# DVE's order in the slots of an attention pair: the turn of exponentials ahead of the move of scores

## The reference

```python
q = x @ Wq.T + bq
p = softmax(q @ memory_keys.T / sqrt(128))          # 8192 x 4096
x = layernorm(x + (p @ memory_values) @ Wo.T + bo)
h = silu((x @ w1.T) * s1) * ((x @ w2.T) * s2)       # width 512
h = gelu((h @ h1.T) * s_h1)
h = gelu((h @ h2.T) * s_h2)
x = layernorm(x + (h @ w3.T) * s3)
```

## Time and profile before

| | |
|---|---|
| median of 3 runs | 1143.17 us (1141.53 to 1144.19) |
| profiled execution, its own time | 1143.68 us |
| its span, first to last instruction | 1141.9 us |
| attention, first frames | 0 to 117 us |
| attention, repeating pairs | 117 to 620 us |
| attention, last pairs | 620 to about 770 us |
| feed-forward | to the end |
| busy over the span | PE 96%, DVE 84%, ACT 79%, POOL 57% |

### The profile page before, as it was taken

How to read it: one execution, slowest core, us unless ns; L and a number is a source line. 1 busy time by engine, 2 the same in 40 slices (tenths; PEclk the granted TensorE clock), 3 DMA queues, 4 the chain that set the end, 5 groups by cost and what they waited for, 6 DMA issues and landing times. The chain is left out here.

```text
span 1141.9 us, 20141 instructions
## 1 busy us (share of the span) xinstructions
PE 1092.9 (96%) x5324; PEld 769.4 (67%) x5324; DVE 963.5 (84%) x1803; ACT 905.3 (79%) x1610; POOL 645.3 (57%) x618
## 2 busy tenths in 40 slices
PE   7799999999999999999999999988999999999996
PEld 5566666666666666666666666635787887888775
DVE  6888898998899889998998899875787887888874
ACT  6788788878887887788878877777788878888883
POOL 1487788878877887888778878760211121121110
PEclk9999999999999999999999999999999999999999
DMA  6878888888888888888888988854020111001000
GB/s 199 190 186 200 200 201 205 206 197 204 201 195 195 202 200 199 200 206 202 200 194 208 207 186 198 186 124 166 1 56 28 28 48 34 28 28 55 11 10 29
DMA packets 83942, 165.90 MB, mean 145 GB/s; under 512 B 19648, under 2 KB 47808, under 8 KB 83776
## 3 DMA queue, kind: packets, MB, share of 16 engines
q1 hardware_dynamic: 79824, 161.50, 59.8%
q10 hardware_dynamic: 4080, 3.94, 1.2%
HBM read 22.76 MB, written 8.39 MB: 27 GB/s over the span
## 5 line engine op out<-in xcount | busy, mean ns | idle before, releaser
L454 POOL TENSOR_TENSOR pT<-slot_p,pT 128x512 f16<-128x512 f32 x496 | 561.9, 1168 | 143.5 <-ACT pT L506 143.5
L608 DVE TENSOR_SCALAR_CACHE_REDUCE rows<-s_ps 128x1024 f32<-128x1024 f32 x256 | 310.8, 1214 | 72.9 <-DMA slot_p<-rows 48.3
L506 ACT ACTIVATE pT<-slot_p 128x512 f16<-128x512 f32 x512 | 296.1, 617 | 84.1 <-DMA slot_p<-rows 76.2
L577 DVE STREAM_TRANSPOSE rows<-rows 128x1024 f32<-128x1024 f32 x256 | 317.0, 1239 | 2.1 <-ACT rows L497 2.1
L497 ACT ACTIVATE rows<-rows,bias 128x1024 f32<-128x1024 f32 x256 | 291.6, 1139 | 15.7 <-DVE bias L616 15.4
L711 PE MATMUL s_ps<-keys,q_buf 128*128 128x512 f32 x512 | 249.6, 488 | 7.7 <-DVE rows L608 4.8
L685 PE MATMUL o_ps<-pT,v_hi 128*128 128x512 f16 x512 | 198.1, 387 | 21.2 <-POOL pT L454 20.9
L990 PE MATMUL ring<-h_hi,w_all 128*128 128x512 f32 x512 | 205.6, 402 | 1.7 <-DVE h_lo L936 1.4
L712 PE MATMUL s_ps<-keys,q_buf 128*128 128x512 f32 x512 | 203.4, 397 | 0.0
L991 PE MATMUL ring<-h_lo,w_all 128*128 128x512 f32 x512 | 202.3, 395 | 0.0
L713 PE MATMUL s_ps<-keys,q_buf 128*128 128x512 f32 x512 | 202.1, 395 | 0.0
(11 more groups left out here) (95 smaller groups left out, 1202.1 us busy)
## 6 DMA issues: line engine op xcount, KB each, us to landing
slot_p<-rows SPq DMA_DIRECT2D x1020, 128.0 KB, 2.4
x_in<-in_xT SPq DMA_DIRECT2D x32, 128.0 KB, 2.5
x_in<-in_x SPq DMA_DIRECT2D x16, 256.0 KB, 3.6
o_scratch<-o_sum SPq DMA_DIRECT2D x32, 128.0 KB, 2.0
out<-y_out SPq DMA_DIRECT2D x16, 256.0 KB, 2.4
o_in<-o_scratch SPq DMA_DIRECT2D x14, 256.0 KB, 3.3
z<-in_w_all ACTq DMA_DIRECT2D x25, 113.0 KB, 3.1
rows<-in_w_all SPq DMA_DIRECT2D x1, 2816.0 KB, 12.5
```

Of the source, the lines that this page charges most:

```text
L454: nc.gpsimd.tensor_tensor(halves(s % RING, 1), slots_first(pp, s), halves(s % RING, 0), ALU.subtract).then_inc(split, 1)
L506: nc.scalar.activation(halves(s % RING, 0), slots_first(pp, s), ACT.Copy).then_inc(highed, 1)
L577: nc.vector.transpose(row_piece(tile, k), row_piece(tile, k)).then_inc(turned, 1)
L608: nc.vector.tensor_scalar(row_piece(tile, k), s_ps[:, j % 2, :], 1.0, None, ALU.mult, ALU.max, accum_out=part_max[:, tile, k:k + 1]).then_ ...
```

## The change

DVE's turn of a slot is put ahead of the wait and the move. Which piece is turned in which slot stays the same, and so do the frames of the other engines. The split of the queries in slot 4 (L602) stays first.

```diff
                     before = turned_piece(f, j)
                     if j == PIECES and valid(f + 1, PAIRS):
                         q_low_part(f + 1, 1 - par)
+                    if valid(before[0], PAIRS):
+                        turn_piece(*before)
                     if valid(f, PAIRS):
 
                         dve.wait_ge(scored, 8 * f + j + 1)
...
                         nc.vector.tensor_scalar(bias[:, tile:tile + 1], row_max[:, tile:tile + 1], -SCALE, None,
                                                 ALU.mult).then_inc(bias_ready, 1)
-                    if valid(before[0], PAIRS):
-                        turn_piece(*before)
                     if is_step(f, 0) and j == PIECES - 1:
```

## The result

The changed kernel runs at 1134.79 us (median of 4 runs, 1134.54 to 1137.6) beside 1142.9 for the kernel before in the same set of runs: ratio 0.9935, 95% interval 0.9915 to 0.9954. By the ratio that is 7.4 us; the two medians lie 8.1 us apart. The forecast was 1136.9 with a range of 1131 to 1144.5. The profiled execution is the slowest of the four, 1137.6 us, with a span of 1135.8 us in place of 1141.9.

What follows compares the result with a forecast made beforehand. It took a loop of waits through SP, DVE, ACT and POOL, varying with piece 2's landing, as the bound, not PE. Check load 4.0, start 1.5 and last pairs 0.8 gave 6.3 us less: 1136.9 us, range 1131 to 1144.5.

Steps and rivals of the forecast that it cites:

- The order of the moves: DVE: one turn still lies between any two moves, so the fixed 11.74 us from move 2 stays: 0 us.
- Turns a slot sooner: SP's 7.2 us of waits on turns go, 0.33 us a pair, but its wait for POOL grows alike: no direct gain.
- The check load: ACT's check load moves forward, away from piece 2, so the head shortens: 0.18 us a pair, 22 pairs, 4.0 us.
- The slope of 1.3 us per us: Head time per shift of the check load: 0.52 us of head for 0.39 us, from the mean head and pair 6.
- The start: Pair 0's last turns come a slot, 2.28 us, sooner, so pair 1's exchange and the loop start sooner: 1.5 us.
- The last pairs: SP's piece 6 of pair 30 waits on a turn and a move 1.21 us for its landing: 0.8 us gained.
- Head of the line: DVE: the turn now first waits for its exponential with the move queued behind it; 0.5 us of slack, so 0 us.
- Slower: Rival, chance 0.10: without SP's pauses piece 2 meets a full DMA queue, head 11.51 us in every pair: 1150.4 us.
- Only the lead: Rival, chance 0.20: the check load's place doesn't matter, only the start and end terms stay: 1140.9 us.
- Every pair as pair 6: Rival, chance 0.12: all 22 pairs get pair 6's head, 0.52 us less each, plus start and end: 1129.5 us.
- SP as the bound: Rival, chance no more than 0.05: SP's sequencer bounds the kernel, so its 7.2 us on turns go at once: 1133.7 us.
- The feedback: A pair shorter by d starts its next exchange sooner by d, making the check load that much later against it; d = 0.19.

Runs made afterwards that it cites:

- after_ck7: The changed kernel with ACT's check load written at step 7 in place of step 3: 1136.37 us, ratio 0.9981 to the kernel before.
- before_ck7: The kernel before, old order, with ACT's check load written at step 7 in place of step 3: 1138.72 us, ratio 1.0003.
- loop_only_again: Third set: the kernel before with the turn first in the loop's frames (4 to 27) alone, run once more: 1137.37 us, ratio 0.9983.
- after_x4_ck7: The changed kernel with the check load at step 7 and SP's load of x in slot 4, not 6: 1125.28 us, ratio 0.9882 to before.
- before_ck8: The kernel before, old order, with the check load written at ACT's step 8, behind its waits there: 1134.18 us, ratio 0.9958.
- after_again: The changed kernel run once more, in the first set, against the kernel before: 1135.44 us, ratio 0.9926.
- start_only: The kernel before with the turn first in frames 0 to 3 alone: 1139.17 us, ratio 0.9971.
- end_only: The kernel before with the turn first in frames 28 to 34 alone: 1141.09 us, ratio 0.9985.
- loop_only: First set: the kernel before with the turn first in the loop's frames (4 to 27) alone: 1139.16 us, ratio 0.9956.
- before_again: The unchanged kernel before, profiled once more in the third set: 1138.41 us, ratio 0.9995.

## Why the prediction was right, and where its terms were off

**Direction, size and range** were right: 6.3 us forecast, 7.4 and 8.5 us measured (8.1 and 7.4 by the medians). That the size came out has luck in it. Its largest term has a mechanism that the runs bear out only in part, the two smaller ones were each put too low by the runs, and in the other two sets the same order gave less: 2.4 us in after_ck7 against before_ck7, 1.9 in loop_only_again, where the first set had 5.0.

**What bounded the kernel.** Right: a loop through SP, the landing of piece 2, DVE's moves 2 and 3, the bias, ACT and POOL, with PE close behind. Removing 0.5 us of issue from the head took 11 us off (after_x4_ck7 against after_ck7), which no PE-bound kernel would give, and PE set the pace of all pairs only once that was gone. One thing was said too strongly: the part behind move 2 isn't fixed. Where the head is 10.2 us it is 12.0, and in before_ck8 12.38.

**The order of the moves, 0 us.** Right in this profile, where the part behind move 2 stayed at 11.73 us. In the three other profiles of the new order it is 11.80 or 11.81, about 0.1 us longer, as move 3 meets its landing behind a short head.

**Turns a slot sooner, no gain in itself.** The "slot" is wrong: the turn passes one move, some 1.2 us, within the same slot. That was enough: SP's pauses on turns went and came back as waits for POOL (13.0 to 18.2 us). The sign given for it, a wait of move 2 below 1 us, isn't seen in this profile (1.21 us in the mean) and is in after_again (0.85).

**The check load, 22 x 0.18 = 4.0 us.** The mechanism stands only in part, and this is the weakest step. What before_ck8 shows is that the load beside piece 2 makes the head longer: at 15 us it fell by 0.86. What isn't shown is that the new order gains by moving the load forward. In this profile the load moved by 0.14 us against piece 0 and the pair got shorter by 0.10; in the first set it moved by less than 0.1 and the pair got shorter by 0.17. The slope of 1.3 us per us came from two pairs, and the other pairs of the same trace don't bear it out: pair 19 has its load at 5.36 us and a head of 10.80, pair 17 at 5.37 and 11.51, pairs 8 and 20 at 5.59 and 5.63 and 10.80 and 10.73. Over the 22 pairs there is no relation between the two (correlation -0.02). Nor is there one in before_ck7, whose load stood 0.7 us later. The forecast reckoned with a mean shift; in three of the four profiles of the new order the gain is in every other pair, with a load at 4.8 to 5.1 us and a head of 10.2 to 10.6. Why the pairs take turns is open.

**The start, 1.5 us.** Undersized by the time: start_only gives 3.3 us (1.8 to 4.7). The traces give it more narrowly. Pair 2 starts at 71.31 to 73.43 us in the eight profiles that start in the old order and at 69.59 to 70.88 in the six that start in the new one, 1.9 us sooner in the mean; in the changed kernel's own profile it is 1.0 (70.62 for 71.66). The turns in question came 1.4 us sooner and not 2.28, for the reason given above, so the upper bound was wrong and the term near all the same. The lead was kept, as said.

**The last pairs, 0.8 us.** end_only gives 1.7 us (0.2 to 3.2), but its profiled execution is no shorter than that of before. Its size stays open, and so does whether it is more than nothing.

**Head of the line, 0 us.** Turns now wait 3.8 us for exponentials in 14 places, at most 0.4 us each. By the forecast that is nearly its sign of being wrong, "by the pair". It costs nothing that can be seen: the waits stand before the turn of piece 3, in slot 0, so in the head, and there move 2 still waits 1.21 us for its landing behind them.

**Rivals.** "Slower" falls: piece 2 doesn't land later. "Only the lead" falls in the first set by loop_only, but it describes the second, where after_ck7 gained 2.4 us on before_ck7 with pairs alike. "Every pair as pair 6" isn't reached, though single pairs go past it (head 10.17 in pair 17). SP as the bound, which gave 1133.7 and was near the measured time, falls for another reason: its waits for POOL grew, and PE's floor, not SP's, ended the gains. The Trainium skill, DMA: Bandwidth & Descriptors, section Issuing engines are not separate DMA queues, says that DMAs of all queues run on the same 16 DMA engines and interleave. The runs agree: the load on ACT's queue slowed pieces 5 and 6 of SP's exchange once it stood beside them, in place of piece 2. But the conclusion that its place doesn't matter doesn't follow: it matters who waits for the piece that is slowed.

## What to carry to other kernels

Follow one loop of waits through all engines and split its period in a part that hardly varies and one that does; the gain lies in what makes the second long, here small loads that stand ahead of the one transfer that everyone waits for, or beside it. Before two pairs are made into a slope, look at all 22. Put such loads in a pause that the issuing queue has anyway, or behind a wait on their own queue, and look in the trace where they were really issued. Measure each variant beside the kernel before in the same set of runs: its own time differed by 4 us between two sets on one chip, half of what was to be measured.

## What the runs showed of the hardware

The sequencer of ACT issued a DMA written at step 7 only 0.7 us later than the one at step 3 (6.17 in place of 5.47 us after piece 0), and 5.7 us ahead of ACT's own copy of that step (441.84 and 447.57 in before_ck7). At step 8, behind two waits, it came at 15.0 us.

A load of 113 KB on ACT's queue slows the pieces of SP's exchange that it stands beside: piece 2 landed 2.73 us after its last issue with the load near it and 1.77 without, pieces 5 and 6 took 0.4 us longer once the load stood beside them (before_again and before_ck8, means of 22 pairs).

The steady pairs of the changed kernel fall into a rhythm of two, 22.2 and 23.2 us, for pairs 15 to 20: a check load 4.88 us after piece 0 goes with a short pair (416.86 - 411.98, head 10.17), and the next pair's load stands at 5.79 us (439.98 - 434.19), and that pair is long (head 11.41). In after_again, loop_only and loop_only_again the rhythm holds for most pairs. The feedback that the forecast put in its sum as an average could give such a rhythm, but that it is the cause isn't shown. In all four profiles it is the odd pairs that are short. The loop holds two frames written out, and SP's issue of pieces 2 to 6 takes 12.95 us in pair 17 and 12.59 in pair 18 without a wait in either, so the two halves of the loop aren't alike to begin with.
